# A cross-attention kernel: attention times weights in four 64x64 tiles of the array

## What is computed

```python
# layer 0, heads of 16 channels (B', C, N, H = 32, 128, 1024, 8)
attn = softmax(einsum('bhni,bhnj->bhij', q, k) * scale);  out = einsum('bhnd,bhde->bhne', v, attn)
res_p2r = xca(heads(rgb, wq_rgb),   heads(geo, wk_point), heads(geo, wv_point)) @ proj_p2r.T
res_r2p = xca(heads(geo, wq_point), heads(rgb, wk_rgb),   heads(rgb, wv_rgb))   @ proj_r2p.T
x1 = rgb + res_p2r + geo + res_r2p            # back in (b, c, n)
# layer 1, q and k from y = ctx, v from x1, softmax over channels of a head
o = conv(Wo, bo, attention(conv(Wq, bq, y), conv(Wk, bk, y), conv(Wv, bv, x1))) + x1
out = (o - mean(o)) * rsqrt(var(o) + eps) * gn_w + gn_b
```

## Time and profile before

| | |
|---|---|
| median of 3 runs | 376.18 us (375.7 to 377.04) |
| the profiled execution | 373.84 us, span 372.0 us |
| PE busy | 345.0 us, 2922 matmul instructions |
| DVE busy | 290.6 us |
| ACT busy | 244.1 us |
| POOL busy | 215.2 us |
| granted TensorE clock, mean | 0.995 of full speed |

### The profile page before, as it was taken

One profiled execution on the slowest core, in us unless ns is written; L12 is line 12 of the kernel. 1 busy time (PEld: TensorE's weight loads), 2 busy tenths in 40 slices (PEclk: granted clock), 3 DMA queues, 4 the chain that ended last, 5 costly groups with the idle time before them and its releaser, 6 DMA issues.

```text
span 372.0 us, 8681 instructions
## 1 busy us (share of the span) xinstructions
PE 345.0 (93%) x2922; PEld 309.2 (83%) x2922; DVE 290.6 (78%) x715; ACT 244.1 (66%) x397; POOL 215.2 (58%) x323
## 2 busy tenths in 40 slices
PE   6979999999999999999999999999999999999882
PEld 3869889898888989888898988889888888997661
DVE  2584778978887897888789788878979787897864
ACT  2775676758587675858767585876758587675522
POOL 0659376682837658283765828376582847658101
PEclk9999999999999999999999999999999999999997
DMA  8734404437341453634144373413427242200222
GB/s 267 304 118 153 183 14 171 157 115 226 113 172 60 168 163 113 226 113 155 72 158 178 113 226 111 166 62 146 192 113 226 108 132 99 113 0 0 115 113 113
DMA packets 14411, 51.58 MB, mean 139 GB/s; under 512 B 1856, under 2 KB 1984, under 8 KB 14400
## 3 DMA queue, kind: packets, MB, share of 16 engines
q1 hardware_dynamic: 14400, 51.44, 39.0%
HBM read 34.66 MB, written 16.78 MB: 138 GB/s over the span
## 4 chain that ended last, share of the span: by engine, by line
PE 73%; DVE 15%; issue 5%; ACT 3%; DMA 2%; SPq 0%; POOLq 0%; POOL 0%; DVEq 0%; ACTq 0%
PE tpy L297 8%; PE oacc L338 7%; PE oacc L333 7%; PE oacc L334 7%; PE gacc L310 7%; PE tpx L284 6%; PE gacc L313 6%; PE gacc L311 5%; DVE mom L679 5%; PE mid L357 4%; PE mid L415 4%; DVE t_lo L642 3%; ACT res L527 2%; PE mid L401 2%; DVE mom L675 2%
## 5 line engine op out<-in xcount | busy, mean ns | idle before, releaser
L906 POOL TENSOR_TENSOR xy_lo<-raw,xy_hi 128x256 fp32r<-128x256 f32 x256 | 178.4, 737 | 17.3 <-ACT xy_hi L520 14.9
L894 POOL TENSOR_TENSOR attn<-probs,sinv 32x192 f32<-32x192 f32 x46 | 25.7, 558 | 97.3 <-DVE sinv L769 95.6
L310 PE MATMUL gacc<-t_hi 128*128 128x258 f32 x256 | 78.0, 305 | 0.6 <-DVE t_lo L642 0.6
L313 PE MATMUL gacc<-t_hi,t_lo 128*128 128x258 f32 x256 | 71.9, 281 | 0.0
L311 PE MATMUL gacc<-t_lo,t_hi 128*128 128x256 f32 x256 | 71.8, 280 | 0.0
L520 ACT ACTIVATE xy_hi<-raw 128x1024 fp32r<-128x1024 f32 x64 | 67.7, 1057 | 0.0
L642 DVE TENSOR_TENSOR t_lo<-tpx,t_hi 128x512 fp32r<-128x512 f32 x64 | 43.8, 684 | 19.2 <-ACT t_hi L484 19.2
L333 PE MATMUL oacc<-xy_hi,pq_hi 128*128 128x512 f32 x124 | 52.7, 425 | 0.7 <-ACT pq_hi L502 0.7
L297 PE MATMUL tpy<-cst,raw 128*128 128x128 f32 x256 | 39.3, 276 | 13.1 <-DVE t_lo L642 11.2
L310 PEld LDWEIGHTS gacc<-t_hi 128*128 128x128 f32 x256 | 48.4, 189 | 2.7 <-issue 0.7
L311 PEld LDWEIGHTS gacc<-t_lo,t_hi 128*128 128x128 f32 x256 | 48.6, 190 | 0.6
(11 more groups left out here) (101 smaller groups left out, 600.6 us busy)
## 6 DMA issues: line engine op xcount, KB each, us to landing
raw<-in_x SPq DMA_DIRECT2D x32, 512.0 KB, 3.4
raw<-in_ctx SPq DMA_DIRECT2D x32, 512.0 KB, 5.2
out<-res SPq DMA_DIRECT2D x32, 512.0 KB, 6.1
wt<-in_weights SPq DMA_DIRECT2D x1, 896.0 KB, 8.5
cst<-in_consts SPq DMA_DIRECT2D x1, 147.0 KB, 3.3
quad<-in_quad_rows SPq DMA_DIRECT2D x1, 32.0 KB, 7.0
vec<-in_vectors SPq DMA_DIRECT2D x1, 2.0 KB, 6.1
```

The lines of the kernel that those rows point to most:

```text
L310: pe.matmul(gacc[:, 0:2 * C + 2], yhi, t_hi[b][:, c, :], start=(c == 0), stop=False)
L313: mm = pe.matmul(gacc[:, 0:2 * C + 2], ylo, t_hi[b][:, c, :], start=False, stop=(c == CH - 1))
L906: piece = pool.tensor_tensor(xy_lo[slot][:, s, cols], raw[slot][:, s, cols], xy_hi[slot][:, s, cols].bitcast(f32), ALU.subtract)
```

## The change

It touches five things.

1. `attn` becomes [128, 6, 64]. Since a matrix is zero off its diagonal blocks, rows 0 to 63 keep only columns 0 to 63, and rows 64 to 127 only columns 64 to 127. The writers on DVE and POOL write to the matching half.
2. z_products replaces six 128x128 by 128-column products by twelve of 64x64 by 128 columns (24 instructions), each in one of four tiles of the array: row half g, column half k. Of two products r = 0, 1 the first uses the tiles (0,0) and (1,1), the second (0,1) and (1,0), so the second's result lands with its two halves of partitions exchanged (rotated by 64). The row half g writes bank g of mid.
3. z_out copies partitions 0 to 63 of both banks in one instruction, and 64 to 127 with the banks in reverse order in another, 768 elements each; one semaphore instead of two. The rotated z needs weights with rotated rows, so two further loads bring `w_rot` (prT and v with the halves exchanged), and m_products has four products instead of three.
4. The wait for attn moves ahead of gram chunk 6 (z_operands).
5. warm_up reads a tile of its own, zeroed first.

```diff
-        attn = sb("attn", [C, 6, C])
+        attn = sb("attn", [C, 6, H64])
+        warm = sb("warm", [C, 4 * C])
-        z = sb("z", [C, 3, 2, C])
+        z = sb("z", [C, 2, 3, C])
-        mid0 = pb("mid0", [C, HALF])
-        mid1 = pb("mid1", [C, HALF])
+        mid = pb("mid", [C, 2, HALF])
+        mid0, mid1 = mid[:, 0, :], mid[:, 1, :]
...
             sp.dma_start(wt[:, :, :], weights).then_inc(weights_in, 16)
+            k = WNAMES.index("prT")
+            sp.dma_start(w_rot[0:H64, :, :], weights[H64:C, k:k + 2, :]).then_inc(weights_in, 16)
+            sp.dma_start(w_rot[H64:C, :, :], weights[0:H64, k:k + 2, :]).then_inc(weights_in, 16)
...
-            def z_products(p):
+            def z_operands(p):

                 pe.wait_ge(attn_dve_ready, p + 1)
                 pe.wait_ge(attn_pool_ready, p + 1)
-                for i, name in enumerate(("vp", "vr", "oT")):
-                    for a in range(2):
-                        dst = mid1[:, (2 * i + a) * C:(2 * i + a + 1) * C] if i < 2 else mid0[:, a * C:(a + 1) * C]
-                        mm = pe.matmul(dst, attn[:, 2 * i + a, :], w(name), start=True, stop=True)
+
+            def z_products(p):
+
+                for s in range(3):
+                    for r in range(2):
+                        i, a, name = ((0, s, "vp"), (1, s, "vr"))[r] if s < 2 else (2, r, "oT")
+                        for g in range(2):
+                            k = g ^ r
+                            rows, cols = slice(H64 * g, H64 * (g + 1)), slice(H64 * k, H64 * (k + 1))
+                            mm = pe.matmul(mid[cols, g, s * C:(s + 1) * C], attn[rows, 2 * i + a, :], w(name)[rows, :],
+                                           start=True, stop=True, tile_position=(H64 * g, H64 * k))
                 mm.then_inc(z_done, 1)
...
-                pe.wait_ge(z12_ready, p + 1)
-                pe.matmul(mid1[:, 0:2 * C], w("ppT"), z[:, 0, :, :], start=True, stop=True)
-                pe.matmul(mid1[:, 2 * C:4 * C], w("prT"), z[:, 1, :, :], start=True, stop=True).then_inc(m12_done, 1)
-                pe.wait_ge(z3_ready, p + 1)
-                pe.matmul(mid0[:, 0:2 * C], w("v"), z[:, 2, :, :], start=True, stop=True).then_inc(m3_done, 1)
+                pe.wait_ge(z_ready, p + 1)
+                pe.matmul(mid1[:, 0:2 * C], w("ppT"), z[:, 0, 0:2, :], start=True, stop=True)
+                pe.matmul(mid1[:, 2 * C:4 * C], w_rot[:, 0, :], z[:, 1, 0:2, :], start=True, stop=True).then_inc(m12_done, 1)
+                pe.matmul(mid0[:, 0:C], w("v"), z[:, 0, 2, :], start=True, stop=True)
+                pe.matmul(mid0[:, C:2 * C], w_rot[:, 1, :], z[:, 1, 2, :], start=True, stop=True).then_inc(m3_done, 1)
...
-                    gram_chunks(h, u, 0, 4, 7)
+                    gram_chunks(h, u, 0, 4, 6)
+                if middle:
+                    z_operands(p - 1)
+                if front:
+                    gram_chunks(h, u, 0, 6, 7)
...
-                act.activation(z[:, 0:2, :, :], mid1[:, :], ACT.Copy).then_inc(z12_ready, 1)
-                act.activation(z[:, 2, :, :], mid0[:, 0:2 * C], ACT.Copy).then_inc(z3_ready, 1)
+                act.activation(z[0:H64, :, :, :], mid[0:H64, :, 0:3 * C].rearrange("p r (s c) -> p r s c", c=C), ACT.Copy)
+                act.activation(z[H64:C, :, :, :], mid[H64:C, ::-1, 0:3 * C].rearrange("p r (s c) -> p r s c", c=C),
+                               ACT.Copy).then_inc(z_ready, 1)
...
-                    last = dve.tensor_tensor(attn[q, :, q], probs[q, :, :],
+                    half = slice(W32 * (j % 2), W32 * (j % 2 + 1))
+                    last = dve.tensor_tensor(attn[q, :, half], probs[q, :, :],
                                              sinv[q, :].unsqueeze(2).broadcast_to([W32, 6, W32]), ALU.mult)
```

More of the change, by code:

```diff
@@ L13 @@
 QUADS = 4
+H64 = C // 2
 W32 = 32
@@ L51, in cross_attention_pair_kernel @@
         wt = sb("wt", [C, len(WNAMES), C])
+        w_rot = sb("w_rot", [C, 2, C])
         vec = sb("vec", [C, len(VNAMES)])
@@ L129, in cross_attention_pair_kernel @@
         attn_zero = sem("attn_zero")
+        warm_set = sem("warm_set")
         ones_set = sem("ones_set")
@@ L155, in cross_attention_pair_kernel @@
         z_done = sem("z_done")
-        z12_ready = sem("z12_ready")
-        z3_ready = sem("z3_ready")
+        z_ready = sem("z_ready")
         m12_done = sem("m12_done")
@@ L265, in warm_up @@
                 for k in range(WARM):
-                    pe.matmul(oacc[0][:, 0:3 * C], attn[:, 0, :], attn[:, 1:4, :], start=True, stop=True)
-            pe.wait_ge(attn_zero, 1)
+                    pe.matmul(oacc[0][:, 0:3 * C], warm[:, 0:C], warm[:, C:4 * C], start=True, stop=True)
+            pe.wait_ge(warm_set, 1)
             warm_up()
@@ L348, in u_products @@
                 if isinstance(p, int) and p == 0:
-                    pe.wait_ge(weights_in, 48)
+                    pe.wait_ge(weights_in, 80)
                     pe.wait_ge(prepared, 6)
@@ L609, in _ @@
         def _(dve):
+            dve.memset(warm[:, :], 0.0).then_inc(warm_set, 1)
             dve.memset(attn[:, :, :], 0.0).then_inc(attn_zero, 1)
@@ L622, in prepare @@
                 dve.wait_ge(consts_in, 16)
-                dve.wait_ge(weights_in, 48)
+                dve.wait_ge(weights_in, 80)
                 s0, s1 = float(C // H) ** -0.5, float(C) ** -0.5
@@ L893, in softmax_out @@
                     q = slice(W32 * j, W32 * (j + 1))
-                    last = pool.tensor_tensor(attn[q, :, q], probs[q, :, :],
+                    half = slice(W32 * (j % 2), W32 * (j % 2 + 1))
+                    last = pool.tensor_tensor(attn[q, :, half], probs[q, :, :],
                                               sinv[q, :].unsqueeze(2).broadcast_to([W32, 6, W32]), ALU.mult)
```

## The result

Over 20 executions of each kernel the median went from 375.92 to 377.48 us. The ratio is 1.0038 with a 95% interval of 1.002 to 1.0056, so the change makes the kernel slower by 0.8 to 2.1 us. The forecast was 376.5 us in a range of 375.0 to 378.0, and most of its chance (0.74) lay on "within 0.3%"; the measured ratio is just past that bound, on the side that had 0.17.

What follows compares the result with a forecast made beforehand. DVE's chain was taken to bound the steady steps, covering the shortened PE block. Steady steps 0, step (0, 1) +0.11, the end +0.17, rest 0: +0.28 on 373.84 profiled gives 374.1, or 376.5 us as median; range 375.0 to 378.0.

Steps and rivals of the forecast that it cites:

- The bound: Steady steps: DVE's chain covers PE's attention-times-weights block; PE's wait at the y transposes grows from 0.72 to about 1.1 us.
- the rival with two tiles at once: Tiled block: two tiles run at once instead of four; together +1.6, 377.7 us; chance 0.10.
- The block: Attention times weights on PE: four tiles at once, 0.64 us plus 0.34 in and out, 0.98 us, 0.36 shorter.
- no overlap: Tiled block: row tiles don't overlap at all; +16.4, 392.6 us; chance 0.06.
- The copies of z: ACT's two copies: 0.82 us each, z ready 1.53 us after z_done; steady-step margin 1.04 us, cost nothing.
- The moved wait: Wait for attn, one gram chunk earlier on PE: margin 1.3 us, cost 0.
- Step (0, 1): Step without out_half and so without DVE's cover: z ready later, +0.11 us.
- Steady steps: The 14 steps under DVE's chain: 14 x 0 = 0, steps stay 21.8 us.
- The end: Step (8, 0), without front: z and the m products' weights later, handed on through nmat, +0.17 us.
- The scale: Whole kernel: timed median 2.3 us above the profiled execution, so the sum of 374.1 becomes 376.5 us.
- PE as the bound: Steady steps: the wait at the y transposes is an artefact, 0.36 us a step comes through; 371.4 us; chance 0.05.
- DVE's chain at another speed: DVE's chain meets POOL's instructions differently: 0.1 us a step either way, 375.1 or 377.9 us; chance 0.11.

Runs made afterwards that it cites:

- both doubled kernels: The kernel before and the changed kernel, each with its attention-times-weights instructions issued twice: 382.99 us (ratio 1.0212) and 378.25 us (ratio 1.0063).
- after_low_stat_split: Changed kernel with low_part of y before DVE's statistics, group_moments behind the m products, attn wait one product ahead, z copied in four parts: 364.02 us, ratio 0.9696.
- after_wait_late: Changed kernel with the wait for attn one gram product ahead of the tiled products instead of three: 377.45 us, ratio 1.0041.
- after_again: The changed kernel timed once more, without further edits: 377.71 us, ratio 1.004.
- after_tail_filled: Changed kernel with two further products of 384 columns behind the tiled block in steps without front, filling PE's idle time in step (8, 0): 376.92 us, ratio 1.0019.

## Why the prediction came out as it did

- **The bound, right.** That the block lies under DVE's chain and that only the wait would grow is what the profile of after and both doubled kernels show. The forecast wait was about 1.1 us; it is 1.10. By the number alone the rival with two tiles at once (377.7 us) would have come nearer to the measured 377.48 than the forecast (376.5); the trace excludes it, and the range would have held either.
- **The block, right.** Forecast 0.98 us, 0.36 shorter. Its 24 instructions pass in 0.82, but 0.09 us of the way in lie in front of them, and the transposes behind take 0.05 more (197.78 to 198.27 in after_low_stat_split, 0.49 instead of 0.44). With 0.82 - 0.64 = 0.18 that makes 0.32 us for the way in and out, where 0.34 was forecast. PE's busy time fell by 0.36 us in the covered stretch and its wait grew by 0.38. Two tiles at once and no overlap are excluded.
- **The copies of z, a wrong step.** The duration was right (0.82 forecast, 0.81 measured). Wrong was the distance: I let the second copy start 0.71 us after the first, since a copy of all partitions starts its successor 0.11 us before its end; the copies of half the partitions start theirs 0.81 to 0.83 us apart. So z needs 1.62 us instead of 1.53, and ACT's further work is later too: 0.43 us of idle time are left in front of the Gram copy, not the forecast 0.64. Covered in the steady steps. In step (0, 1) it didn't show in PE's times either: z's first copy starts 0.66 us sooner behind the block's first product (0.95 instead of 1.61 us), since part of the way in lies in front of that product and the untiled block there started behind a short wait of its own, for POOL.
- **The moved wait, wrong in one step.** I computed its margin (1.3 us) in a steady step and called it 0 for all. Step (0, 1) has no out_half in front, PE comes to chunk 6 sooner, and POOL isn't done; in the kernel before the block itself started only 0.15 us after POOL. Term 0, measured 0.25 (after_wait_late).
- **Steady steps, 0 forecast, 0.02 in one pair of profiles.** In 14 steps it makes 0.3 us of the difference between these two profiles. Profiles of the same steady code differ by 0.01 to 0.015 us a step, and on average the two sorts lie 0.01 us apart, so whether the fourth m product costs anything (0.02 at worst, by the prediction) isn't shown.
- **Step (0, 1), +0.11 forecast, +0.79 measured** at ACT's copy, 0.14 of it given back in the next step. This is the term that was mis-sized. The forecast looked at z alone, and for z nothing was lost (2.63 against 2.64 us). What it left out lies in front of the block, 0.5 us: the moved wait (0.25), and the one product and the way in that lie behind POOL (0.28). Another 0.1 stands behind the wait for z.
- **The end, +0.17 forecast, +0.15 measured, and the clock missed.** That PE's idle time in step (8, 0) would double was in my own numbers (z_done 0.50 earlier, L345 no earlier). I took it for free. In some executions the clock falls to 1.2 GHz there, which costs 1.4 us in the profiled cases, and the executions above 380 us had the lowest mean clocks. What it is worth in the median stays open: after_again and after_tail_filled are 0.8 us apart, within their intervals.
- **The scale.** I noted that the median stood 2.3 us above the profiled execution and carried that on as a constant. A good part of it is the start: 15.67 us in that profile, where full clock came early, up to 17.8 in others of the same kernel's variants. The sum was right to be made as a difference, but a comparison of two single profiles would have said 2.9 us.
- **Rivals.** PE as the bound: excluded. DVE's chain at another speed: L698 takes 1.33 us as L679 did, nothing moved. The measured +1.1 us behind the first copy against the forecast +0.3 is a miss of 0.8 us. It is small against the range and large against the bound of 0.3% to which the chances were given; with step (0, 1) not looked at for every edit, 0.17 for slower was too little.

## What to carry to other kernels

Before an engine's work is made shorter, look at the next wait behind it on that engine and at what ends it: if it is another engine's chain that doesn't read the work, the gain goes into that wait, and the chain's order is the thing to change (here one moved call brought 8.5 us; the tiles brought about 2 only after a second reordering and with earlier copies of z). Then cost the edit in the steps that lack the cover, each with its own margins, since there the side costs (a later release, a wait moved ahead) are all that is left. And idle time given to TensorE near a stretch that is thin already isn't free: it can cost the clock.

## What the runs showed of the hardware

- 64x64 tiles in fp32: 12 products of 128 moving columns (24 instructions) in 0.82 us, where two tiles at once would take 1.28 and four 0.64 (estimates from 0.107 us for one product alone), although the tiles lie in two halves of the rows only. For the scores, whose tiles all have the same rows, four ran at once as well. The rule of the Trainium skill (TensorE: Matmul & The Clock Gate, Part 3, section The mechanism) that a weight load overlaps running products only where its row group differs isn't borne out here.
- The way into and out of 64x64 tiles took some 0.32 us of PE's time: 0.09 in front of the first product, 0.18 within the block and 0.05 behind it.
- ACT copies of 64 partitions with 768 or 512 elements take as long as copies of 128 partitions (0.81 us, where 0.60 for 512 and 0.38 for 256 give 0.82; and 0.59), and their successors start 0.81 to 0.83 and 0.60 us later, where a full copy of 512 lets the next begin after 0.49.
- A wait costs PE more than its listed length: four transposes take 0.44 us of the chain in a run and 0.66 behind a wait, and 0.92 us of added products vanished in a listed wait of 0.72.
- In the start the same four transposes took 0.66 us with full clock on record from 6.2 us on and 1.11 us with it from 10.9 us on.
- The granted clock fell to 1.2 GHz in two of four profiles in which PE had waited some 0.7 us for attn, worked 0.8 us and waited 1.40 us again, and stood at 2.4 GHz through the same place when the last wait was filled with products. Why it falls in one execution and not in the next stays open.
